# The first cross attention of a gated two-layer block: rewritten stage, weights quantised by two comparisons

## The chip, the cores and the metric
One core of one Trainium2 chip runs the whole program. The time is device microseconds for one execution; the median of 3 runs stands in the table below. The trace is one further execution, recorded by the hardware profiler.

## What is computed
Four parts follow each other; each adds tanh(gate) times its result to the rows x, of shape [4, 512, 512]. The change lies in the first part, and in the quantisation of the second part's weights, which this stage does as well:

```python
# 1: cross attention without projections of the queries; ctx is [4, 512, 128]
xn  = (x - mean(x)) / sqrt(var(x) + 1e-5)          # per row of 512
kv  = ctx @ W_k.T + b_k                            # [4, 512, 128]
out = einsum('bij,bjd->bid', xn, kv)               # the rows weigh the keys
sim = einsum('bid,bjd->bij', out, kv) * 512**-0.5
sim = (sim - mean(sim)) * rsqrt(var(sim) + 1e-6) * gamma + beta
x   = x + tanh(g_xattn[0]) * softmax(sim)
# weights of part 2 (w1 and w2, 2048 x 512 each), used as they come out of this:
m   = clip(mean(abs(w)), 1e-5)
q   = clip(round(w / m), -1, 1)                    # -1, 0 or 1, times m later
# 2: feed-forward with 8-bit activations; 3: grouped attention; 4: gated feed-forward
```

## The kernel before
The rows lie in SBUF as 16 tiles of 128 rows by 512 (`xs`), four tiles a batch. `xattn0` is one block of instruction streams, one per engine, each in program order; the engines wait for each other through semaphores, and `ffn0` begins when all of them have left the block. No planner orders the work: the order is the one in which the code issues it.

Batch 0 is peeled, and a hardware loop runs over the other three. In `head(b)` DVE takes the row statistics (`bn_stats` L430, `bn_aggr` L433), POOL forms the inverse root (L523), and DVE writes the normalised rows `xn` (L440). In `project(b)` PE forms the keys (L586), turns them (L589) and the rows (L596, f32 transposes through two PSUM banks that ACT empties, L547), and forms the outputs (L603); `similarities(b)` forms four tiles of 128 x 512 (L611). In `tail(b)` DVE takes statistics of the four similarity tiles (L448), subtracts the mean and multiplies by gamma (L455), multiplies by the inverse root and adds beta (L460), takes the maximum (L464), and, after ACT's exponentials (L554), adds the weighted result to the rows (L472). DVE does `head(b + 1)` and then `tail(b)`.

The weights come as eight chunks of 128 x 2048 f32 (`wf`). ACT sums their magnitudes, two chunks a batch (`magnitudes`, L562). When all eight are summed, DVE and PE form the two scales. Each chunk is then quantised in three passes: multiply by the inverse scale and add 1.5 * 2^23, which rounds (`scale_chunks`, L71 and L73); clip (`clip_chunks`, DVE, L79); subtract the constant and write bf16 (`store_chunks`, L87, L89, L91). `SCALED_BY` and `STORED_BY` say which engine does which chunk. `tail(3)` stands ahead of DVE's share of this; POOL's scaling of three chunks runs beside `tail(3)`.

Of the kernel before, what the change touches and what calls it, by code (L numbers as in the profile page):

```python
# [255 lines left out]
def flamingo(nc, a, out):  # L256
    ctx = ExitStack()
    with ctx:
# [17 lines left out]
        x_loaded = sem("x_loaded")  # L276
# [43 lines left out]
def xattn0(nc, a, ph, sb, ps, sem, g):  # L320
# [14 lines left out]
    W_CHUNKS = 8  # L335
# [16 lines left out]
    bn2 = t("bn2", [P, TILES, 6])
    mv2 = t("mv2", [P, TILES, 2])
    ve2 = t("ve2", [P, TILES])
    rs2 = t("rs2", [P, TILES])
    nmax = t("nmax", [P, TILES])
    esum = t("esum", [P, TILES])
    rsum = t("rsum", [P, TILES])
    wabs = t("wabs", [P, W_CHUNKS])
    b1c, b1d, b1p = t("b1c", [P, INNER // P]), t("b1d", [P, 2, INNER // P]), t("b1p", [P, 3, INNER // P], bf16)  # L360
    b1_loaded, b1_parted, b1_left, b1x_cleared = s("b1_loaded"), s("b1_parted"), s("b1_left"), s("b1x_cleared")
    wtot = t("wtot", [P, 2])
    winv = t("winv", [P, 2])

    xT_ps = [ps(f"a_xTps{k}", [P, SEQ], where=ph) for k in range(2)]
    kv_ps = ps("a_kvps", [P, SEQ], where=ph)
    o_ps = ps("a_ops", [P, SEQ], where=ph)
    sim = ps("a_sim", [P, TILES, SEQ], where=ph)

    kv_loaded, vec_loaded, w_loaded = s("kv_loaded"), s("vec_loaded"), s("w_loaded")  # L370
    x0_loaded = s("x0_loaded")
    passed = s("dve_passed")
    step = s("dve_step")
    ve_ready, rs_ready = s("ve_ready"), s("rs_ready")
    ve2_ready, rs2_ready = s("ve2_ready"), s("rs2_ready")
    xn_ready = s("xn_ready")
    kvT_done, kvT_ready, kvt_done, kv_ready = s("kvT_done"), s("kvT_ready"), s("kvt_done"), s("kv_ready")
    xT_done, xT_ready = s("xT_done"), s("xT_ready")
    o_done, oT_ready = s("o_done"), s("oT_ready")
    sim_done, sim_read = s("sim_done"), s("sim_read")  # L380
    v_ready, exp_ready = s("v_ready"), s("exp_ready")
    wabs_ready, wtot_asked, wtot_done, w_scale_ready = s("wabs_ready"), s("wtot_asked"), s("wtot_done"), s("w_scale_ready")
    chunk_stage = [s(f"chunk_stage{k}") for k in range(W_CHUNKS)]
    SCALED_BY = ("vector", "scalar", "pool", "vector", "scalar", "pool", "scalar", "pool")
    STORED_BY = ("pool", "scalar", "scalar", "pool", "scalar", "pool", "vector", "vector")
    targets = ([w1q[:, k, :] for k in range(CH)]
               + [w2q[:].rearrange("p c n -> p (c n)")[:, k * INNER:(k + 1) * INNER] for k in range(W_CHUNKS - CH)])
    chunks = [wf[:, k, :] for k in range(W_CHUNKS)]
    factors = [winv[:, k // CH:k // CH + 1] for k in range(W_CHUNKS)]

    with nc.Block() as block:

        @block.sync
        def _(sp):
            sp.dma_start(xs[:, 0:TILES, :], g["x_view"][:, 0:TILES, :]).then_inc(x0_loaded, 16)
            sp.dma_start(ident[:], a["identity"]).then_inc(consts_loaded, 16)
            sp.dma_start(gate4[:], a["gates"].rearrange("(o n) -> o n", o=1).broadcast_to([P, 4])).then_inc(consts_loaded, 16)
# [4 lines left out]
            sp.dma_start(gamma[:], a["gamma"].rearrange("(o n) -> o n", o=1).broadcast_to([P, SEQ])).then_inc(vec_loaded, 16)  # L402
            sp.dma_start(beta[:], a["beta"].rearrange("(o n) -> o n", o=1).broadcast_to([P, SEQ])).then_inc(vec_loaded, 16)
            sp.dma_start(xs[:, TILES:, :], g["x_view"][:, TILES:, :]).then_inc(x_loaded, 16)
            w1_view, w2_view = a["w1T"].rearrange("(c p) n -> p c n", p=P), a["w2T"].rearrange("(c p) n -> p c n", p=P)
            for k in range(W_CHUNKS // 2):
                if k:
                    sp.wait_ge(w_loaded, 16 * k)
                if k < 2:
                    sp.dma_start(wf[:, 2 * k:2 * k + 2, :], w1_view[:, 2 * k:2 * k + 2, :]).then_inc(w_loaded, 16)  # L410
                else:
                    sp.dma_start(wf[:, 2 * k:2 * k + 2, :].rearrange("p k (c n) -> p (k c) n", n=DIM),
                                 w2_view[:, IC // 2 * (k - 2):IC // 2 * (k - 1), :]).then_inc(w_loaded, 16)
            sp.dma_start(g["b2g"][:], a["b2"].rearrange("(o n) -> o n", o=1).broadcast_to([P, DIM])).then_inc(g["vec0_loaded"], 16)
            sp.wait_ge(b1_parted, 3)
            sp.wait_ge(b1x_cleared, 1)
            for k in range(3):
                for j in range(3):
                    row = HD * k + j
                    sp.dma_start(g["b1x"][row:row + 1, :].rearrange("o (p n) -> o p n", p=P),  # L420
                                 b1p[:, k, :]).then_inc(g["b1x_loaded"], 16)

        @block.vector
        def _(dve):
            small = Tally(step)

            def head(b, first):

                for i in range(TILES):
                    last = small.mark(nc.vector.bn_stats(bn[:, i, :], xs[:, ds(b * TILES + i, 1), :]))  # L430
                held(dve, step, last, passed)
                for i in range(TILES):
                    last = small.mark(nc.vector.bn_aggr(mv[:, i, :], bn[:, i, :]))  # L433
                dve.wait_ge(step, last)
                nc.vector.tensor_scalar(ve[:], mv[:, :, 1], EPS_IN, None, ALU.add).then_inc(ve_ready, 1)
                if not first:
                    dve.wait_ge(xT_done, b * CH)
                dve.wait_ge(rs_ready, b + 1)
                for i in range(TILES):
                    last = nc.vector.tensor_scalar(xn[:, i, :], xs[:, ds(b * TILES + i, 1), :],  # L440
                                                   mv[:, i, 0:1], rs[:, i:i + 1], ALU.subtract, ALU.mult)
                last.then_inc(xn_ready, 1)

            def tail(b):

                for i in range(TILES):
                    dve.wait_ge(sim_done, b * TILES + i + 1)
                    last = small.mark(nc.vector.bn_stats(bn2[:, i, :], sim[:, i, :]))  # L448
                held(dve, step, last, passed)
                for i in range(TILES):  # L450
                    last = small.mark(nc.vector.bn_aggr(mv2[:, i, :], bn2[:, i, :]))
                dve.wait_ge(step, last)
                nc.vector.tensor_scalar(ve2[:], mv2[:, :, 1], EPS_SIM, None, ALU.add).then_inc(ve2_ready, 1)
                for i in range(TILES):
                    nc.vector.scalar_tensor_tensor(out=v[:, i, :], in0=sim[:, i, :], scalar=mv2[:, i, 0:1],  # L455
                                                   in1=gamma[:], op0=ALU.subtract, op1=ALU.mult).then_inc(sim_read, 1)
                dve.wait_ge(rs2_ready, b + 1)
                for i in range(TILES):
                    dve.wait_ge(sim_read, b * TILES + i + 1)
                    last = small.mark(nc.vector.scalar_tensor_tensor(  # L460
                        out=v[:, i, :], in0=v[:, i, :], scalar=rs2[:, i:i + 1], in1=beta[:],
                        op0=ALU.mult, op1=ALU.add))
                    dve.wait_ge(step, last)
                    nc.vector.tensor_reduce(nmax[:, i:i + 1], v[:, i, :], axis=AX, op=ALU.max,  # L464
                                            negate=True).then_inc(v_ready, 1)
                dve.wait_ge(exp_ready, b * TILES + TILES)
                last = small.mark(nc.vector.reciprocal(rsum[:], esum[:]))
# [1593 lines left out]
```

## Time and profile before

| | us |
|---|---|
| median of 3 runs | 921.85 (921.52 to 922.08) |
| the profiled execution | 921.24, of which the recorded span is 919.3 |
| the changed block in the trace | 0.7 to 128.7 |
| busy in the whole span: PE, DVE, ACT, POOL | 674.5, 703.1, 598.3, 330.4 |

The block's end is the end of POOL's last store at L91. The first instruction of `ffn0` starts at 129.0. Times in the views are counted from the start of the span.

### The profile page before, as it was taken

The page shows a single profiled execution, that of the slowest core. Times are in us where ns is not written, and L with a number is a line of the kernel's source. Part 1 is how long each engine was busy: PE and PEld are TensorE (multiplying, and loading weights), DVE is VectorE, ACT ScalarE, POOL GpSimd, SP SyncE. Part 2 cuts the span into 40 slices and gives each one's busy share as a digit, 9 for nine tenths or more (in the row PEclk, how much of TensorE's full clock was granted, in tenths as well). Part 3 has the DMA queues.
Part 4 walks back from the last instruction along what each step waited for, and adds up shares of the span by engine and source line. Part 5 has one row for each costly group of instructions (what it writes and reads, how often), then busy time and mean ns, then how long its engine had stood idle before and what let it go on. Part 6 is the DMA issues. An engine that isn't in the chain of part 4 may idle for free. (4 is left out here: it accounts for less than half of the span.)

```text
span 919.3 us, 14368 instructions
## 1 busy us (share of the span) xinstructions
PE 674.5 (73%) x5260; PEld 374.0 (41%) x5260; DVE 703.1 (76%) x1170; ACT 598.3 (65%) x784; POOL 330.4 (36%) x353
## 2 busy tenths in 40 slices
PE   4655007676857774769989887999998477879796
PEld 2322003333323332435654555465555144545453
DVE  3886977999999999687785589476451478989884
ACT  2546428999795989378884688399554055656574
POOL 1110460343468556365283167021112013323232
PEclk9977557999797997869999998999999888989899
DMA  8710030000000000432231012022100000000001
GB/s 330 260 46 0 0 118 20 1 0 1 1 1 0 1 1 1 134 105 89 77 113 32 1 65 76 13 86 70 36 2 1 32 1 0 35 24 23 23 36 46
DMA packets 21726, 43.68 MB, mean 48 GB/s; under 512 B 3872, under 2 KB 8480, under 8 KB 20768
## 3 DMA queue, kind: packets, MB, share of 16 engines
q1 hardware_dynamic: 21664, 42.85, 13.7%
q8 instruction: 39, 0.64, 0.3%
q14 instruction: 23, 0.19, 0.1%
HBM read 38.61 MB, written 4.19 MB: 47 GB/s over the span
## 5 line engine op out<-in xcount | busy, mean ns | idle before, releaser
L1338 DVE TENSOR_REDUCE c_nmax<-c_s 128x1 f32<-128x384 f32 (+3 forms) x176 | 108.6, 633 | 83.6 <-PE c_s L1548 83.4
L1450 ACT ACTIVATE c_probs<-c_e 128x512 f32<-128x512 f32 (+1 forms) x176 | 94.4, 558 | 56.7 <-PE c_e L1578 55.6
L1046 PE MATMUL b_y<-w2q,b_q2T 128*128 128x512 bf16 x256 | 72.6, 438 | 53.5 <-ACT b_q2T L971 28.0
L1273 POOL TENSOR_TENSOR c_psum<-c_probs 128x1536 f32<-128x1536 f32 x16 | 55.8, 3490 | 155.7 <-ACT c_probs L1450 155.7
L1976 PE MATMUL d_gu<-gateq,d_xqT 128*128 128x352 bf16 x512 | 94.8, 336 | 13.4 <-DVE d_h L1777 12.4
L1545 PE MATMUL c_s<-c_kT,c_qaT 96*128 96x128 f16 (+3 forms) x256 | 73.8, 321 | 19.7 <-DVE c_nmax L1338 18.2
L1020 PE MATMUL b_up<-shared,b_xqT 128*128 128x512 bf16 x256 | 71.3, 404 | 2.6 <-ACT b_h L937 2.6
L1576 PE MATMUL c_e<-c_qaT,c_kT 98*128 98x512 f16 (+3 forms) x256 | 69.7, 306 | 4.1 <-ACT c_qaT L1437 3.6
L1905 ACT ACTIVATE d_sg<-d_gu,d_dq 128x352 f32<-128x352 f32 x64 | 35.3, 553 | 53.9 <-PE d_gu L1976 53.9
L1976 PEld LDWEIGHTS d_gu<-gateq,d_xqT 128*128 128x128 bf16 x512 | 49.8, 103 | 50.1 <-DVE d_h L1777 18.3
L1046 PEld LDWEIGHTS b_y<-w2q,b_q2T 128*128 128x128 bf16 x256 | 25.8, 108 | 92.2 <-issue 39.3
L1548 PE MATMUL c_s<-c_mask,ident_b 128*128 128x128 bf16 x256 | 53.5, 233 | 0.0
L1545 PEld LDWEIGHTS c_s<-c_kT,c_qaT 96*128 96x128 f16 x256 | 25.9, 102 | 65.5 <-DVE c_nmax L1338 38.9
L1007 PE MATMUL b_t<-ident_b,b_xq 128*128 128x128 bf16 x80 | 8.7, 251 | 58.9 <-DVE b_inv L757 45.9
L1578 PE MATMUL c_e<-ident_b,c_mask 128*128 128x128 bf16 x256 | 50.5, 223 | 0.0
L1777 DVE SCALAR_TENSOR_TENSOR d_h<-d_gu,d_dq,d_sg 128x352 f32<-128x352 f32 x64 | 37.0, 578 | 9.9 <-ACT d_sg L1905 9.5
L1999 PE MATMUL d_y<-downq,d_q2T 128*128 128x512 bf16 x176 | 41.6, 385 | 3.9 <-ACT d_q2T L1930 3.9
L230 POOL TENSOR_TENSOR c_xsin<-c_xw,ssin 128x256 f32<-128x256 f32 x32 | 32.8, 1043 | 22.5 <-DVE c_xw L214 22.5
L766 DVE SCALAR_TENSOR_TENSOR b_h<-b_h,b_nmu,b_ln_g 128x2048 f32<-128x2048 f32 x16 | 37.6, 2349 | 3.5 <-ACT b_nmu L946 3.4
L1860 POOL TENSOR_SCALAR d_q<-d_h 128x1408 bf16<-128x1408 f32 x16 | 23.0, 1438 | 47.0 <-ACT d_h L1920 46.9
L774 DVE SCALAR_TENSOR_TENSOR b_h<-b_h,b_rstd,b_ln_b 128x2048 f32<-128x2048 f32 x16 | 38.1, 2379 | 2.4 <-POOL b_rstd L876 2.4
L1020 PEld LDWEIGHTS b_up<-shared,b_xqT 128*128 128x128 bf16 x256 | 26.0, 104 | 34.0 <-issue 11.1
(233 smaller groups left out, 1849.4 us busy)
## 6 DMA issues: line engine op xcount, KB each, us to landing
c_stage<-in_gateT SPq DMA_DIRECT2D x16, 704.0 KB, 4.1
c_stage<-in_downT SPq DMA_DIRECT2D x6, 768.0 KB, 4.4
a_wf<-in_w1T SPq DMA_DIRECT2D x2, 2048.0 KB, 13.3
a_wf<-in_w2T SPq DMA_DIRECT2D x2, 2048.0 KB, 8.3
out<-xs SPq DMA_DIRECT2D x16, 256.0 KB, 2.0
xs<-in_x SPq DMA_DIRECT2D x1, 3072.0 KB, 14.8
xs<-in_x SPq DMA_DIRECT2D x1, 1024.0 KB, 5.3
a_ctxT<-in_ctxT SPq DMA_DIRECT2D x1, 1024.0 KB, 7.2
```

Source lines behind the costliest of these rows:

```text
L774: nc.vector.scalar_tensor_tensor(out=h2[:, n % H2S, :], in0=h2[:, n % H2S, :], scalar=rstd[:, n:n + 1], in1=ln_b[:], op0=ALU.mult, op1=ALU ...
L1020: nc.tensor.matmul(up_ps[k][:, m * DIM:(m + 1) * DIM], xqT[:, n % 4, c, :], w1q[:, c, at:at + DIM], start=(c == 0), stop=False)
L1046: last = nc.tensor.matmul(y_ps[:], q2T[:, n % 2, c, :], w2q[:, c, :], start=(c == 0), stop=(c == IC - 1))
L1273: nc.gpsimd.tensor_tensor(psum[:], region(slot, 0)[:, :, P:], region(slot, 1), ALU.add).then_inc(psum_ready, 1)
L1338: nc.vector.tensor_reduce(nmax[:, G % 2, i, n:n + heads], s_ps[u % 2][:, 0:heads * (i + 1) * P].rearrange("p (n k) -> p n k", n=heads), ax ...
L1450: nc.scalar.activation(probs[:, G % 2, at:at + width], e_ps[fill % 3][:, 0:width], ACT.Exp).then_inc(e_read, 1)
L1545: nc.tensor.matmul(s_ps[u % 2][:, m * width:(m + 1) * width], qaT[0:AUG, grp * GROUP + n + m, i * P:(i + 1) * P], kT[0:AUG, b % 2, grp, 0: ...
L1548: last = nc.tensor.matmul(s_ps[u % 2][:, m * width + i * P:(m + 1) * width], ident_b[:], mask[:], start=False, stop=True)
L1576: nc.tensor.matmul(e_ps[fill % 3][:, m * width:(m + 1) * width], kT[0:FULL, b % 2, grp, k * P:(k + 1) * P], qaT[0:FULL, h + m, k * P:], st ...
L1578: last = nc.tensor.matmul(e_ps[fill % 3][:, m * width:m * width + P], mask[:], ident_b[:], start=False, stop=True)
L1976: last = nc.tensor.matmul(gu_ps[k % 2][:, half, 0:PART], xqT[:, i % 2, c, :], gateq[:, c, at:at + PART], start=(c == 0), stop=(c == CH - 1))
L1999: last = nc.tensor.matmul(y_ps[:], q2T[:, c, :], downq[:, c, :], start=(c == 0), stop=(c == NC1 - 1))
```

## The change
The block is rewritten without hardware loops.

- The mean of the similarities goes away, because the keys are centred first: ACT sums the keys while it copies them, DVE subtracts the mean (`centred`), and both the values and the similarities use the centred keys. The rows are turned as they were loaded, not normalised. Their inverse deviation cancels in the second normalisation, up to the small constant, which `least` takes up.
- The variance of a similarity tile is a sum of squares by ACT (`square`).
- DVE multiplies a tile by the inverse root and gamma (`sloped`), then adds beta and takes the extreme in one instruction (`shifted`, `tensor_tensor_reduce`).
- Work on tiles is ordered by pairs, with six slots for `v`, four PSUM banks for similarities, two copies of keys, values and outputs. The fronts of the next batches are issued ahead.
- A transposed row block is emptied from PSUM 1024 wide, two instructions a batch.
- A weight becomes (w > m/2) - (w < -m/2): POOL writes the second comparison to the bf16 target (`below`), DVE the first minus it (`ternary`). ACT has no part in it. Chunks 0 to 3 need only the first scale.
- SP issues all loads at once without waits between the weight chunks, the context first, the rows by batch.

Core of the diff (added lines; those they replace are in the functions above):

```diff
+            def centred(b):
+                dve.wait_ge(kvT_ready, b + 1)
+                last = small.mark(nc.vector.tensor_scalar(kmean[:, b:b + 1], ksum[:, b:b + 1], 1.0 / SEQ, None, ALU.mult))
+                dve.wait_ge(step, last)
+                if b >= 2:
+                    dve.wait_ge(sim_done, (b - 1) * TILES)
+                nc.vector.tensor_scalar(kvcT[:, b % 2, :], kvT[:], kmean[:, b:b + 1], None, ALU.subtract).then_inc(kvc_ready, 1)
+            def variances(p):
+                dve.wait_ge(squared, 2 * p + 2)
...
+            def sloped(n):
+                dve.wait_ge(rs_ready, n // 2 + 1)
+                if n >= SLOTS:
+                    dve.wait_ge(x_ready, n - SLOTS + 1)
+                nc.vector.scalar_tensor_tensor(out=v[:, n % SLOTS, :], in0=sim[n % SIMS][:], scalar=rs[:, n:n + 1], in1=gamma,
+                                               op0=ALU.mult, op1=ALU.mult).then_inc(sim_read, 1)
+            def shifted(n):
+                dve.wait_ge(sim_read, n + 1)
+                at = v[:, n % SLOTS, :]
+                nc.vector.tensor_tensor_reduce(at, at, beta, -1.0, 3.0e38, ALU.add, ALU.min, nmax[:, n:n + 1]).then_inc(v_ready, 1)
...
+            def finished(p):
+                shares(p)        # waits for exponentials 2p and 2p+1
+                residual(2 * p)
+                residual(2 * p + 1)
...
+            def ternary(k):
+                dve.wait_ge(below_ready, k + 1)
+                nc.vector.scalar_tensor_tensor(out=targets[k], in0=wf[:, k, :], scalar=over[:, k // CH:k // CH + 1], in1=targets[k],
+                                               op0=ALU.is_gt, op1=ALU.subtract).then_inc(quantised, 1)
...
+            for b in range(BATCH):
+                variances(2 * b)
+                if b == 0:
+                    centred(1)
+                elif b + 2 < BATCH:
+                    centred(b + 2)
+                variances(2 * b + 1)
+                if b == 0:
+                    bias_parts()
+                else:
+                    finished(2 * b - 1)
+                if b == 2:
+                    weight_scale(0)
+                for p in range(2 * b, 2 * b + 2):
+                    for n in (2 * p, 2 * p + 1):
+                        sloped(n)
+                    for n in (2 * p, 2 * p + 1):
+                        shifted(n)
+                if b == 0:
+                    centred(2)
+                if b + 1 < BATCH:
+                    statistics(b + 1)
+                if b == 3:
+                    ternary(0)
+                    weight_scale(1)
+                    ternary(1)
+                finished(2 * b)
+                if b == 1:
+                    weight_sum(0)
+                if b == 2:
+                    weight_sum(1)
+            ternary(2)
+            finished(PAIRS - 1)
+            for k in range(3, W_CHUNKS):
+                ternary(k)
...
         @block.gpsimd
+            def below(k):
+                pool.wait_ge(under_ready, k // CH + 1)
+                nc.gpsimd.tensor_scalar(targets[k], wf[:, k, :], under[:, k // CH:k // CH + 1], 1.0,
+                                        ALU.is_lt, ALU.mult).then_inc(below_ready, 1)
...
+            for p in range(PAIRS):
+                pool.wait_ge(ve_ready, p + 1)
+                nc.gpsimd.tensor_tensor(rs[:, cols(p)], ve[:, cols(p)], minus_half[:, 0:2], ALU.pow).then_inc(rs_ready, 1)
+                if p == 5:
+                    below(0)
+                    below(1)
+                if p == 6:
+                    below(2)
+            for k in range(3, W_CHUNKS):
+                below(k)
...
         @block.scalar          # MAGNITUDES = (((), (0, 1)), ((2,), (3, 4)), ((5, 6), (7,)), ((), ()))
+            front_out(0)       # keys_out, rows_out(b, 0), values_out, rows_out(b, 1), outputs_out
+            for b in range(BATCH):
+                for n in range(b * TILES, (b + 1) * TILES):
+                    square(n)
+                if b == 0:
+                    act.wait_ge(consts_loaded, 16)
+                    nc.scalar.activation(gate4[:], gate4[:], ACT.Tanh).then_inc(gates_ready, 1)
+                    front_out(1)
+                if b + 2 < BATCH:
+                    keys_out(b + 2)
+                    rows_out(b + 2, 0)
+                for k in MAGNITUDES[b][0]:
+                    magnitude(k)
+                exponential(b * TILES)
+                exponential(b * TILES + 1)
+                if b + 2 < BATCH:
+                    values_out(b + 2)
+                    rows_out(b + 2, 1)
+                exponential(b * TILES + 2)
+                exponential(b * TILES + 3)
+                for k in MAGNITUDES[b][1]:
+                    magnitude(k)
+                if b + 2 < BATCH:
+                    outputs_out(b + 2)
...
         @block.tensor          # front(b): keys, turn_rows(b, 0), turn_keys, turn_rows(b, 1), outputs
+            front(0)
+            for b in range(BATCH):
+                for n in range(b * TILES, (b + 1) * TILES):
+                    similar(n)
+                if b == 0:
+                    front(1)
+                if b + 2 < BATCH:
+                    front(b + 2)
+                if b >= 2:
+                    weight_total(b - 2)
```

## Rows read from the trace of the kernel before

**Rows 1.** The page, part 1: busy time, share, instructions of each engine.
```profile
PE 674.5 (73%) x5260; PEld 374.0 (41%) x5260; DVE 703.1 (76%) x1170; ACT 598.3 (65%) x784; POOL 330.4 (36%) x353
```

**Rows 2.** Stretches of 10 us: length, busy time of each engine, granted clock, DMA.
```profile
60.00:70.00 10.00, 1.70 (x6) 0.57 (x4) 8.06 (x20) 5.47 (x8) 1.01 (x1) 0.76 0.00 0
...
110.00:120.00 10.00, 0.00 (x0) 0.00 (x0) 10.00 (x10) 5.51 (x3) 6.93 (x1) 0.50 0.00 0
120.00:130.00 10.00, 0.00 (x0) 0.00 (x0) 3.85 (x5) 0.00 (x0) 9.21 (x4) 0.50 0.01 2
```

**Rows 3.** The timeline to 80 us: start, length, engine, line, operation.
```profile
10.43 2.07 PE L586 MATMUL a_kvps<-a_ctxT,a_wkT 128*128 128x512 f32 x2 [10.43 <-DMA a_ctxT<-in_ctxT]
...
17.68 3.60 PE L603 MATMUL a_ops<-a_xT,a_kv 128*128 128x512 f32 x8
...
21.96 3.70 PE L611 MATMUL a_sim<-a_kvT,a_oT 128*128 128x512 f32 x8 [0.69 <-ACT a_oT L549]
...
42.06 2.47 DVE L430 BATCH_NORM_STATS2 a_bn<-xs 128x6 f32 x4
...
63.70 2.46 DVE L430 BATCH_NORM_STATS2 a_bn<-xs 128x6 f32 x4
...
73.63 4.54 PE L603 MATMUL a_ops<-a_xT,a_kv 128*128 128x512 f32 x8
```

**Rows 4.** Groups of instructions in 0 to 200 us: busy us, mean ns | idle before.
```profile
L562 ACT ACTIVATE a_junk<-a_wf 128x2048 bf16 (+1 forms) x8 | 15.2, 1904 | 0.6
...
L596 PE MATMUL a_xTps<-ident,a_xn 128*128 128x128 f32 x64 | 13.1, 382 | 8.2 <-DVE a_xn L440 7.9 <-ACT a_xT L547 0.3
L554 ACT ACTIVATE a_v<-a_v,a_nmax 128x512 f32<-128x512 f32 x16 | 11.5, 718 | 8.2 <-DVE a_nmax L464 8.0
...
L464 DVE TENSOR_REDUCE a_nmax<-a_v 128x1 f32<-128x512 f32 x16 | 11.0, 686 | 0.5
L472 DVE SCALAR_TENSOR_TENSOR xs<-a_v,a_rsum,xs 128x512 f32 (+1 forms) x16 | 11.0, 746 | 0.5 <-DVE a_rsum L469 0.5
L937 ACT ACTIVATE b_h<-b_up,b_dq 128x1024 f32<-128x1024 f32 x10 | 10.9, 1113 | 3.4 <-PE b_up L1022 3.4
L455 DVE SCALAR_TENSOR_TENSOR a_v<-a_sim,a_mv,a_gamma 128x512 f32<-128x512 f32 x16 | 10.9, 742 | 0.0
...
L448 DVE BATCH_NORM_STATS2 a_bn<-a_sim 128x6 f32<-128x512 f32 x16 | 9.9, 681 | 0.0
L430 DVE BATCH_NORM_STATS2 a_bn<-xs 128x6 f32 (+1 forms) x16 | 9.9, 679 | 5.0 <-DMA xs<-in_x 5.0
...
L547 ACT ACTIVATE a_xT<-a_xTps 128x512 f32<-128x512 f32 x16 | 9.3, 597 | 11.7 <-PE a_xTps L596 11.6
...
L440 DVE TENSOR_SCALAR a_xn<-xs,a_mv,a_rs 128x512 f32 (+1 forms) x16 | 7.7, 543 | 4.6 <-POOL a_rs L523 4.6
...
L554 ACT ACTIVATION_READ_ACCUMULATOR a_v<-a_v,a_nmax 128x1 f32 x16 | 3.0, 189 | 0.0
```

**Rows 5.** The timeline from 94 us, POOL, then DVE.
```profile
96.00 6.72 POOL L73 TENSOR_SCALAR a_wf<-a_wf,a_winv 128x2048 f32<-128x2048 f32 x3
113.07 13.75 POOL L91 TENSOR_SCALAR shared<-a_wf 128x2048 bf16<-128x2048 f32 x2 [10.35 <-DVE a_wf L79]
126.80 1.89 POOL L91 TENSOR_SCALAR w2q<-a_wf 128x2048 bf16<-128x2048 f32 x1
...
99.15 1.74 DVE L460 SCALAR_TENSOR_TENSOR a_v<-a_v,a_rs,a_beta 128x512 f32<-128x512 f32 x1
...
120.85 2.35 DVE L89 TENSOR_SCALAR w2q<-a_wf 128x2048 bf16<-128x2048 f32 x2
```

**Rows 6.** Single lines of the program: duration in ns, least/median/most, and starts.
```profile
L73 POOL TENSOR_SCALAR a_wf<-a_wf,a_winv x3: 1969/2394/2395, 96.0 to 100.3; 128x2048 f32<-128x2048 f32 x3
...
L766 DVE SCALAR_TENSOR_TENSOR b_h<-b_h,b_nmu,b_ln_g x16: 2339/2344/2403, 150.7 to 354.6; 128x2048 f32<-128x2048 f32 x16
```

**Rows 7.** The page, part 5: the costliest two-tensor operation on POOL.
```profile
L1273 POOL TENSOR_TENSOR c_psum<-c_probs 128x1536 f32<-128x1536 f32 x16 | 55.8, 3490 | 155.7 <-ACT c_probs L1450 155.7
```

More of the change, by code:

```diff
@@ L376, in xattn0 @@
[L376 to L383, printed above, removed]
@@ L425, in _ @@
             small = Tally(step)
[L427 to L433, printed above, removed]
-                dve.wait_ge(step, last)
[L435 to L451, printed above, removed]
-                dve.wait_ge(step, last)
[L453 to L467, printed above, removed]
-                dve.wait_ge(step, last)
-                last = small.mark(nc.vector.tensor_scalar(rsum[:], rsum[:], gate4[:, 0:1], None, ALU.mult))
-                dve.wait_ge(step, last)
-                for i in range(TILES):
-                    last = small.mark(nc.vector.scalar_tensor_tensor(
-                        out=xs[:, ds(b * TILES + i, 1), :], in0=v[:, i, :], scalar=rsum[:, i:i + 1],
-                        in1=xs[:, ds(b * TILES + i, 1), :], op0=ALU.mult, op1=ALU.add))
@@ new lines, in statistics @@
+            def statistics(b):
+                dve.wait_ge(rows_loaded[b], 16)
+                for n in range(b * TILES, (b + 1) * TILES):
+                    last = small.mark(nc.vector.bn_stats(bn[:, n, :], xs[:, n, :]))
+                dve.wait_ge(step, last)
+                for n in range(b * TILES, (b + 1) * TILES):
+                    last = small.mark(nc.vector.bn_aggr(mv[:, n, :], bn[:, n, :]))
+                dve.wait_ge(step, last)
+                c = slice(b * TILES, (b + 1) * TILES)
+                nc.vector.tensor_scalar(least[:, c], mv[:, c, 1], SPREAD, SPREAD * EPS_IN, ALU.mult, ALU.add).then_inc(least_ready, 1)
@@ new lines, in shares, with residual @@
+            def shares(p):
+                c = cols(p)
+                dve.wait_ge(exp_ready, 2 * p + 2)
+                last = small.mark(nc.vector.reciprocal(rsum[:, c], esum[:, c]))
+                dve.wait_ge(step, last)
+                last = small.mark(nc.vector.tensor_scalar(share[:, c], rsum[:, c], gate4[:, 0:1], None, ALU.mult))
+                dve.wait_ge(step, last)
+            def residual(n):
+                nc.vector.scalar_tensor_tensor(out=xs[:, n, :], in0=v[:, n % SLOTS, :], scalar=share[:, n:n + 1], in1=xs[:, n, :],
+                                               op0=ALU.mult, op1=ALU.add).then_inc(x_ready, 1)
@@ new lines, in outputs_out, with square, exponential @@
+                nc.scalar.activation(oT[:, b % 2, :], o_ps[:], ACT.Copy).then_inc(oT_ready, 1)
+            def square(n):
+                act.wait_ge(sim_done, n + 1)
+                if n:
+                    act.wait_ge(squared, n)
+                nc.scalar.activation(junk2[:], sim[n % SIMS][:], ACT.Square, accum_out=squares[:, n:n + 1]).then_inc(squared, 1)
+            def exponential(n):
+                act.wait_ge(v_ready, n + 1)
+                at = v[:, n % SLOTS, :]
+                nc.scalar.activation(at, at, ACT.Exp, bias=nmax[:, n:n + 1], scale=-1.0, accum_out=esum[:, n:n + 1]).then_inc(exp_ready, 1)
@@ L580, in _, with keys, turn_keys @@
         @block.tensor
         def _(pe):
-            def project(b, first):
-                if not first:
+            def keys(b):
+                if b:
                     pe.wait_ge(kv_ready, b)
-                nc.tensor.matmul(kv_ps[:], wkT[:], ctxT[:, ds(b * SEQ, SEQ)], start=True, stop=True).then_inc(kvT_done, 1)
+                nc.tensor.matmul(kv_ps[:], wkT[:], ctxT[:, b * SEQ:(b + 1) * SEQ], start=True, stop=True).then_inc(kvT_done, 1)
+            def turn_keys(b):
+                pe.wait_ge(kvc_ready, b + 1)
@@ L600, in project, with similar @@
                     pe.wait_ge(oT_ready, b)
                 for c in range(CH):
[L602 to L603 removed]
+                    last = nc.tensor.matmul(o_ps[:], kv[:, b % 2, c, :], xT[:, c, :], start=(c == 0), stop=(c == CH - 1))
                 last.then_inc(o_done, 1)
[L606 removed]
+            def similar(n):
+                b, i = n // TILES, n % TILES
@@ L607, in similarities @@
                 pe.wait_ge(oT_ready, b + 1)
-                for i in range(TILES):
-                    if not first:
-                        pe.wait_ge(sim_read, b * TILES - TILES + i + 1)
-                    nc.tensor.matmul(sim[:, i, :], oT[:, i * P:(i + 1) * P], kvT[:], start=True, stop=True).then_inc(sim_done, 1)
-            pe.wait_ge(kv_loaded, 48)
-            pe.wait_ge(consts_loaded, 32)
-            project(0, True)
-            similarities(0, True)
-            with pe.Fori(0, BATCH - 1) as b:
-                project(b + 1, False)
-                similarities(b + 1, False)
@@ new lines, in weight_total, with front @@
+            def weight_total(w):
+                pe.wait_ge(wtot_ready, w + 1)
+                pe.wait_ge(kv_ready, BATCH)
+                nc.tensor.matmul(kv_ps[:, w:w + 1], ones[:], wtot[:, w:w + 1], start=True, stop=True).then_inc(wtot_done, 1)
+            pe.wait_ge(kv_loaded, 48)
+            pe.wait_ge(ident_loaded, 16)
+            def front(b):
+                keys(b)
+                turn_rows(b, 0)
+                turn_keys(b)
+                turn_rows(b, 1)
+                outputs(b)
```

281 lines of the change are left out of this document (135 added, 146 removed).

## The prediction
> **What bounds the kernel now.** I read the page's busy shares first. No engine is busy for more than 76% of the span (DVE) [rows 1], so the bound changes from stage to stage, and the stage that changes has to be read by itself. The table of stretches shows two kinds of time in it. In the batches DVE is busy 8.06 of 10 us and PE 1.70 [rows 2]; the timeline gives their period, 63.70 - 42.06 = 21.6 us from one batch's row statistics to the next [rows 3]. Per batch DVE's seven groups of 512-wide work make about 4 x (0.68 + 0.54 + 0.68 + 0.74 + 0.74 + 0.69 + 0.75) = 19.3 us by their means [rows 4], so DVE bounds the batches. At the end comes the quantisation. From 110 us DVE is busy 10.00 of 10 us, then 3.85, while POOL is busy 9.21 [rows 2]. The timeline says why: two POOL stores take 13.75 us, from 113.07 to 126.8; DVE's last instruction of the block ends at 120.85 + 2.35 = 123.2; POOL's third store, alone, takes 1.89 us, and its end, 128.7, is the block's [rows 5]. The second of the two stores began after that, so the first took 13.75 - 1.9 = 11.9 us for work that costs 1.89 alone, because DVE worked back to back beside it. The block thus ends with POOL locked out and finishing alone.
>
> **What the lock does.** The new form puts two-input DVE work beside POOL work, so this price decides. L460 has two SBUF inputs; beside POOL's L73 one of them took 1.74 us, while L455, with one input in PSUM, keeps a mean of 0.74 [rows 4, 5]. L73 itself took 1.969 us the first time and 2.394 after that [rows 6]. 2.394 - 1.969 is nearly the part of a 512-wide operation that streams. Both read as exclusion: one runs, the other stands, and only some 0.2 us of start-up overlaps. Serial prices follow. A POOL pass of 2048 costs about 1.83 us (1.89 alone), a 512-wide two-input DVE operation 0.68, a 2048-wide one 2.27 (2.344 alone, less start-up) [rows 4 to 6].
> The Trainium skill (SBUF — State Buffer, Who interferes with whom) states this as a rule: a DVE instruction with two SBUF inputs and a POOL instruction that reads SBUF take turns, for the whole instruction. By that rule, eight `below` and eight `ternary` are hardly parallel; the trace agrees (1.74 against 0.74 us). Without it the sum would be the one of rival C.
>
> **Part by part, before the last stage.** Removed from DVE: similarity statistics (16 x 0.68), the normalised rows (16 x 0.54), the separate maximum (16 x 0.69) [rows 4]: 30.6 us. Added: centring (4 x about 0.8, from a 512-wide L440 plus a small operation), 16 accumulator outputs, and the eight `ternary`, 18.2 us, in place of 12 DVE passes (L73, L79, L89) at 1.2 us (L89, 2.35 for two [rows 5]), 14.1 us. So DVE's own work shrinks by only some 20 us (30.6 + 14.1 - 3.2 - 2.7 - 18.2), and less of it may be seen, since ACT gains work: 16 squares at 0.9 us (0.718 + 0.189, taken from the exponential; the lower bound is a copy from PSUM plus the accumulator, 0.6 + 0.19) [rows 4]. ACT loses its six quantisation passes, some 11 us.
>
> *First similarity.* Now at 21.96 [rows 3]. The context was behind the rows in the queue and landed at 10.43; it will be ahead, and PE begins near 8. Keys 2.2, half of the rows turned 1.8 (16 transposes of mean 0.38 overlap to about 0.22 each) [rows 4], keys turned, the other half 1.8, one 1024-wide copy 1.1 on each side of it (L937) [rows 4], outputs 3.6, copy 0.6: about 20.5. The fourth square ends near 25.1. DVE's start waits for the tanh of the gates, which is behind those squares, so 25.3 is DVE's start.
>
> *Squares of batch 1.* The chain runs through PE and ACT. 25.3 -> keys out 0.9, DVE centres 0.8, keys and rows turned 1.8, copy 1.1: 29.9 -> outputs 3.6, keys(2) 1.0: 34.5 -> ACT keys and rows out 2.1: 36.7 -> two exponentials 1.8 (DVE finished them by 31), values 0.6, rows 1.1: 40.2. PE then makes outputs(2) and the similarities by 47.5, because these stand behind front(2) in its queue. ACT is later: two exponentials 1.8, two magnitudes 4.2 (1.904 + 0.189 each), outputs 0.6, four squares 3.6: 50.4. DVE idles about 7 us here.
>
> *Squares of batch 2.* 50.4 -> keys out 0.9; DVE centres, then variances, `finished(1)` 1.9, two `sloped` and two `shifted` 2.8: 56.9 -> ACT exponentials to 58.0, values and rows out 1.7: 59.7. From here ACT needs 1.8 + 4.2 + 0.6 to 66.3, and PE 3.6 at full clock, 4.54 at the mixed clock that L603 met once after an idle stretch [rows 3], plus one similarity of 0.95: 64.3 to 66. Four squares: 70.3. A slower clock is hidden under ACT here.
>
> **The last stage, from 70.3.** DVE now has a queue of work without gaps, each term with its serial price. Not through the shared port: eight `sloped` (one input in PSUM) 8 x 0.68 = 5.4, the last row statistics 3.2, five pairs of shares 2.3, variances 0.5, scales 1.2: 12.6. Through it: eight `shifted` at 0.85 = 6.8, ten `residual` at 0.68 = 6.8, eight `ternary` 18.2: 31.8. POOL's `below` 4 to 7 come when DVE has nothing else than port work: 4 x 1.83 = 7.3. `below` 0 to 3 (7.3 in all) lie beside `sloped` and statistics for about half; I count 3.5. Sum 55.2, end 125.5.
> `shifted` is an operation that no row shows. Its main pass is bounded below by L460's 0.68 and above by L460 and L464 apart, 0.74 + 0.69; I take the lower plus 0.17 for an accumulator read, as ACT's 0.189. With the upper, ten of them on the path cost 5.8 more; with nothing for the accumulator, 1.7 less. `below` has no row either, as a comparison: from 1.83 (L91, the same widths and types) up to 2048/1536 x 3.49 = 4.65 (L1273, two tensors [rows 7]). I take 1.83, being the row of the same operation.
>
> **Forecast.** The block ends at 125.5 instead of 128.7: 3.2 us less. Everything behind the block keeps its order and tiles; I cost it at nothing. PE stands idle before `ffn0` both times and the granted clock is at 1.2 GHz there already (0.50) [rows 2]. So the profiled execution goes from 921.24 to 918.0, and the median, 0.6 higher than the profiled one, from 921.85 to 918.6. About 0.2% (1.8 us) is what can be told from no change here. My own range for this case is 915 to 921.5: the ends of `shifted`, start-up 1 us either way, `below` 0 to 3 shown from 1 to 6 us.
>
> **Rivals.**
> A. *POOL's comparison is dear* (the other side). A compare is slower on POOL than the add and multiply of L91. All eight `below` lie under the lock or ahead of a waiting `ternary`, so each us of extra length costs near 8 us. At 3.3 us each, the middle of the bounds, that is 8 x 1.5 = 12 more: 930.6. It decides from 1.83 + (1.8 + 3.2)/8 = 2.5 us; beneath that the result is not slower by 0.2%. For it: no comparison of POOL in the trace. Against: L91 and L73 do two arithmetic operations with different outputs at the same price. Chance 0.13.
> B. *The early chain is longer.* ACT and PE lead in the first 70 us; one exponential, copy or wait more in each of the two cycles, and idle time that I packed too tightly, give 3 to 6 us: 921.6 to 924.6, say 922.5. For it: many crossings of semaphores; against: DVE's idle time there absorbs what DVE does. Chance 0.16.
> C. *POOL runs beside DVE after all.* Then `below` costs nothing, 10.8 us less: about 908. Rows 5 speak against it. Chance 0.07.
> D. *The fused add and extreme runs at half rate.* 0.53 us more for each `shifted`, ten on the path: 923.9. For it is only that L460 with two f32 inputs has no accumulator; L766 at 2.344 us for 2048 elements shows full rate without one [rows 6]. Chance 0.06.
> The Trainium skill has a rule of this kind (Vector Engine (DVE) Microarchitecture Reference, Points that are easy to get wrong: "`S2S2D2_STT` with two non-bf16 SBUF sources halves throughput"). Taken for plain operations the trace disagrees (2.344 us is one element a cycle of 1.04 ns); with an accumulator no run shows it yet.
> E. *It doesn't do what it says*: PE still waits long, DVE does not shed its gaps, and the block ends within 1.8 us of before. Chance 0.06, at 921.5.
>
> **Chances.** Forecast 0.52, of which faster 0.42, same 0.10. B: 0.04 faster, 0.07 same, 0.05 slower. C faster 0.07. A slower 0.13. D 0.02 same, 0.04 slower. E 0.01 faster, 0.03 same, 0.02 slower. Sums: faster 0.54, same 0.22, slower 0.24. The likeliest is 918.6. The range goes down to 913, half way to C, since overlap of `below` could be better than counted, and up to 926, past B and D and short of most of A.
>
> **What would show it right or wrong.** The timeline should show the first similarity near 20.5, square 7 ending near 50, square 11 near 70, DVE without a gap over 1 us after that, and the last `ternary` near 125. Pairs of `below` and `ternary` should add up to about 4.1 us each, with PE idle and DVE and POOL never both streaming. `below` alone in its line should show a least duration near 1.9, `shifted` 0.74 plus a short read. If `below` shows over 2.5 us, A holds and the forecast fails; if DVE ends `ternary` 7 before 120, C; if square 11 ends after 74, B.

## The result, and the profile after

| | median us | ratio to before, same chip (95% interval) | block ends at, us |
|---|---|---|---|
| before | 921.68 (4 runs) | | 128.7 |
| changed | 938.13 (4 runs) | 1.0179 (1.0161 to 1.0197) | 145.3 |

I forecast 918.6 in a range of 913 to 926; the change makes the kernel 1.8% slower. The profiled execution took 938.19 us against 921.24, 16.95 more, and the block ends 145.3 - 128.7 = 16.6 us later. So the loss lies inside the rewritten block, and what stands behind it moved by no more than 0.4 us.

Where it goes is seen first in the stretches of 10 us of the changed kernel (length, busy time of PE, its weight loads, DVE, ACT, POOL, then granted clock and DMA), to be laid beside [rows 2]:

```profile
60.00:70.00 10.00, 6.27 (x15) 2.79 (x14) 4.22 (x14) 7.79 (x14) 2.30 (x3) 0.84 0.00 0
70.00:80.00 10.00, 7.15 (x8) 2.13 (x8) 9.97 (x18) 5.38 (x11) 10.00 (x2) 0.55 0.00 0
...
110.00:120.00 10.00, 0.00 (x0) 0.00 (x0) 9.96 (x4) 0.00 (x0) 10.00 (x2) 0.50 0.00 0
120.00:130.00 10.00, 0.00 (x0) 0.00 (x0) 9.93 (x4) 0.00 (x0) 10.00 (x3) 0.50 0.00 0
130.00:140.00 10.00, 0.00 (x0) 0.00 (x0) 10.00 (x5) 0.00 (x0) 5.36 (x1) 0.50 0.00 0
```

DVE looks as busy as before, but a count of 4 instructions in 10 us says that it isn't working: an instruction that waits for the port counts as busy. POOL, at 10.00 with two instructions, sets the pace. The timeline of the changed kernel gives both sides (start, length, engine, line):

```profile
69.10 15.23 POOL L565 TENSOR_SCALAR shared<-a_wf,a_under 128x2048 bf16<-128x2048 f32 x2 [1.44 <-DVE a_under L508]
...
70.29 3.94 DVE L468 CUSTOM_DVE_ANT_0 a_v<-a_v,c_turned 128x512 f32<-128x512 f32 x1
74.16 0.08 DVE L468 DVE_READ_ACCUMULATOR2_ANT a_nmax<- 128x1 f32 x1
74.16 0.68 DVE L468 CUSTOM_DVE_ANT_0 a_v<-a_v,c_turned 128x512 f32<-128x512 f32 x1
...
80.22 4.13 DVE L439 TENSOR_SCALAR a_least<-a_mv 128x4 f32<-128x4 f32 x1
81.67 2.68 DVE L473 RECIPROCAL a_rsum<-a_esum 128x2 f32<-128x2 f32 x1
...
103.92 31.44 POOL L565 TENSOR_SCALAR w2q<-a_wf,a_under 128x2048 bf16<-128x2048 f32 x4 [1.25 <-DVE a_under L508]
...
106.07 0.16 DVE L473 RECIPROCAL a_rsum<-a_esum 128x2 f32<-128x2 f32 x1
106.26 6.93 DVE L475 TENSOR_SCALAR a_share<-a_rsum,gate 128x2 f32<-128x2 f32 x1
113.23 5.70 DVE L479 SCALAR_TENSOR_TENSOR xs<-a_v,a_share,xs 128x512 f32<-128x512 f32 x2
118.86 2.34 DVE L513 SCALAR_TENSOR_TENSOR shared<-a_wf,a_over,shared 128x2048 bf16<-128x2048 f32 x1
...
136.17 9.13 DVE L513 SCALAR_TENSOR_TENSOR w2q<-a_wf,a_over,w2q 128x2048 bf16<-128x2048 f32 x4
```

L565 is `below`. Single durations of its line in the changed kernel (ns, least/median/most, first and last start), against 1969/2394/2395 in [rows 6]:

```profile
L565 POOL TENSOR_SCALAR shared<-a_wf,a_under x4: 7156/7308/8053, 69.1 to 95.5; 128x2048 bf16<-128x2048 f32 x4
L565 POOL TENSOR_SCALAR w2q<-a_wf,a_under x4: 7151/7530/9253, 103.9 to 128.2; 128x2048 bf16<-128x2048 f32 x4
```

The shortest comparison pass takes 7.15 us where I had put 1.83. Everything else came near its mark: first similarity at 20.38 (20.5 forecast), the squares of batch 1 done at 47.6 (50.4), those of batch 2 (square 11 is the last of them) at 66.7 (70.3), `shifted` 0.68 with an accumulator read of 0.08, `ternary` 2.34.

### The profile page after: what moved, and what is told of

The parts are those of the page before. It is cut to its first block and busy times, and to the rows that moved or that the text cites. A ratio compares the mean times of both kernels' runs of the same rounds, so it can differ in the third digit from the quotient of the medians.

```text
span 936.4 us, 14250 instructions
## 1 busy us (share of the span) xinstructions
PE 675.8 (72%) x5262; PEld 371.5 (40%) x5262; DVE 715.6 (76%) x1142; ACT 595.4 (64%) x806; POOL 367.0 (39%) x355
## 5 line engine op out<-in xcount | busy, mean ns | idle before, releaser
L1120 PE MATMUL b_up<-shared,b_xqT 128*128 128x512 bf16 x256 | 73.2, 412 | 2.4 <-ACT b_h L1037 2.4
L1029 ACT ACTIVATE b_xqT<-b_t 128x640 bf16<-128x640 bf16 x16 | 11.1, 697 | 66.9 <-PE b_t L1107 66.9
L1678 PE MATMUL c_e<-ident_b,c_mask 128*128 128x128 bf16 x256 | 50.4, 222 | 0.0
L1877 DVE SCALAR_TENSOR_TENSOR d_h<-d_gu,d_dq,d_sg 128x352 f32<-128x352 f32 x64 | 37.0, 578 | 10.2 <-ACT d_sg L2005 9.8
## 6 DMA issues: line engine op xcount, KB each, us to landing
a_wf<-in_w2T SPq DMA_DIRECT2D x2, 2048.0 KB, 20.5
```

What stands on the lines that cost most here:

```text
L1120: nc.tensor.matmul(up_ps[k][:, m * DIM:(m + 1) * DIM], xqT[:, n % 4, c, :], w1q[:, c, at:at + DIM], start=(c == 0), stop=False)
L1678: last = nc.tensor.matmul(e_ps[fill % 3][:, m * width:m * width + P], mask[:], ident_b[:], start=False, stop=True)
L1877: nc.vector.scalar_tensor_tensor(out=h[:, i % 2, k * PART:(k + 1) * PART], in0=gu_ps[k % 2][:, 1, 0:PART], scalar=dq1[:, i:i + 1], in1=sg[ ...
```

## The experiments

Three theories were set against each other. Theory 1: one price is wrong, the comparison on POOL. Theory 2: handing the shared port back and forth costs, whatever POOL does. Theory 3: the rewritten attention loses. The first four kernels ran on one chip, where before took 922.84.

**e1_pool_add.** The comparison becomes an addition.

```diff
 nc.gpsimd.tensor_scalar(targets[k], wf[:, k, :], under[...], 1.0,
-                        ALU.is_lt, ALU.mult)
+                        ALU.add, ALU.mult)
```

> The changed kernel with the comparison in POOL's `below` replaced by an addition, same operands, types and lock; the weights of the second part are then not the reference's. Theory 1 (the comparison itself is dear on POOL, 7.15 us at the least in the trace of the changed kernel against 1.89 for the add and multiply of L91; nothing else failed): `below` falls to 1.9 us alone, the block ends near 121 us instead of 145.3 (my 125.5 less the 4 us by which the squares of batch 2 came earlier), and the time is 914 us. Theory 2 (the handing over of the shared port between POOL and DVE is what costs, small DVE instructions included, whatever POOL does): `below` gets cheaper but gaps and stretched DVE instructions remain, and the block ends at 128 or later, 921 us or more. Theory 3 (the rewritten attention loses the time): 930 us or more.

Measured: 914.97 us, ratio 0.9908 (0.9891 to 0.9926). The same line in this kernel, and its timeline behind square 11:

```profile
L565 POOL TENSOR_SCALAR w2q<-a_wf,a_under x4: 1966/2396/4072, 95.8 to 104.1; 128x2048 bf16<-128x2048 f32 x4
```

```profile
82.53 1.97 POOL L565 TENSOR_SCALAR shared<-a_wf,a_under 128x2048 bf16<-128x2048 f32 x1
82.62 1.89 DVE L455 SCALAR_TENSOR_TENSOR a_ve<-a_squares,a_least 128x2 f32<-128x2 f32 x1 [0.86 <-ACT c_xsin L611]
...
95.76 10.77 POOL L565 TENSOR_SCALAR w2q<-a_wf,a_under 128x2048 bf16<-128x2048 f32 x4 [8.29 <-DVE a_under L508]
...
98.11 1.75 DVE L475 TENSOR_SCALAR a_share<-a_rsum,gate 128x2 f32<-128x2 f32 x1
...
112.64 9.13 DVE L513 SCALAR_TENSOR_TENSOR w2q<-a_wf,a_over,w2q 128x2048 bf16<-128x2048 f32 x4
```

One operation code of one instruction moves the time by 23 us, and the sign of the change with it. The block ends at 121.8. Theory 1 holds in its number (914); theories 2 and 3 fall as the main cause.

**e2_dve_both.** POOL has no part in the quantisation.

```diff
 def ternary(k):
+    nc.vector.tensor_scalar(targets[k], wf[:, k, :], under[...], 1.0, ALU.is_lt, ALU.mult).then_inc(below_ready, 1)
     dve.wait_ge(below_ready, k + 1)
```

> The changed kernel with both comparisons on DVE: `below` is a DVE tensor_scalar right ahead of each `ternary`, POOL has only the inverse roots. Theory 1: no POOL pass and no lock, DVE gets 8 more passes, at 1.22 us each if a comparison runs at the rate of L79 or 2.3 us at one element a cycle; from 66.6 us 44.4 us of DVE work plus 9.8 (or 18.4) end the block near 121 (or 129), 914 (or 922) us. Theory 2 says the same as or better than the run with the addition, since the lock is gone: 8 us or more below it. Theory 3: 930 us or more.

Measured: 912.01 us, ratio 0.9892 (0.9867 to 0.9917), block end 118.4. The timeline's pair for one chunk:

```profile
104.01 1.28 DVE L512 TENSOR_SCALAR w2q<-a_wf,a_under 128x2048 bf16<-128x2048 f32 x1
105.33 2.35 DVE L515 SCALAR_TENSOR_TENSOR w2q<-a_wf,a_over,w2q 128x2048 bf16<-128x2048 f32 x1
```

The comparison that takes POOL 7.15 us takes DVE 1.28. The kernel is 3 us faster than e1, with intervals that overlap, where theory 2 asked for 8 or more; but square 11 is done at 65.5 here and at 68.4 in e1, and from there to the block's end the two need 52.9 and 53.4 us. That is not the price of the lock, since the work differs. DVE does eight passes of 1.28 us more in e2, 10.2 us, and in e1 its instructions behind square 11 last 11.1 us longer than they do alone, because they wait for POOL (L475 1.75 instead of 0.23 us, for one). So the eight short POOL passes cost about what the forecast had put for them, 7.3 + 3.5 = 10.8 us, and little is left over for a price of handing the port back and forth.

**e3_old_quant** and **e4_old_attn** do one part each, as nearly as can be. In e3 `ternary` and `below` become the three passes of before:

```diff
-nc.vector.scalar_tensor_tensor(out=targets[k], in0=wf[:, k, :], scalar=over[...], in1=targets[k], op0=ALU.is_gt, op1=ALU.subtract)
+nc.scalar.activation(wf[:, k, :], wf[:, k, :], ACT.Copy, scale=winv[...], bias=MAGIC)      # 0, 1, 3, 4, 6, 7; POOL 2, 5
+nc.vector.tensor_scalar(wf[:, k, :], wf[:, k, :], MAGIC + 1.0, MAGIC - 1.0, ALU.min, ALU.max)
+nc.gpsimd.tensor_scalar(targets[k], wf[:, k, :], -MAGIC, 1.0, ALU.add, ALU.mult)          # 0, 1, 3, 4, 6; ACT 2, 5, 7
```

> One part undone: the rewritten attention of the changed kernel, the quantisation in the three passes of before (multiply and add, clip, subtract), chunk 2's and 5's first pass on POOL, the others on ACT; POOL writes chunks 0, 1, 3, 4, 6, ACT the others, DVE clips all eight at 1.22 us. Theory 1: the rewritten attention is worth its forecast and more, DVE has 26.2 + 9.8 us from 66.6, ACT and POOL finish after its last clip: block end near 108, time 901 us. Theory 3: the block ends no earlier than 128, 921 us or more.

Measured: 905.65 us, ratio 0.9817 (0.9801 to 0.9833), block end 109.6; theory 3 falls, and the time is 4.7 us over theory 1's. The three passes are shared out otherwise than in the kernel before: there DVE does 12 of the 24 (two multiply and add, eight clip, two store), here only the eight clips. The run is thus not the rewritten attention alone.

In e4 the kernel before gets `over` and `under` in place of `winv`, and:

```diff
-scale_chunks(...); clip_chunks(...); store_chunks(...)
+for k in range(W_CHUNKS):     # POOL; then DVE's second comparison on each
+    nc.gpsimd.tensor_scalar(targets[k], wf[:, k, :], under[...], 1.0, ALU.is_lt, ALU.mult)
```

> The other part alone: the attention of the kernel before, the weights by two comparisons, `below` of all eight chunks on POOL from the scales at 91.5 us, `ternary` on DVE after the last batch's tail. Theory 1: eight passes of 7.15 us on POOL from 96 us with DVE's work between them end near 160, and the ternary passes left over end near 170 to 175: 964 us. Theory 2: the passes on POOL are stretched by the handing over and not long themselves: 935 to 945 us. Theory 3 (the comparisons are cheap, the attention loses): 925 us or less.

Measured: 955.06 us, ratio 1.0346 (1.0328 to 1.0363). From the end of its timeline:

```profile
129.81 28.58 POOL L534 TENSOR_SCALAR w2q<-a_wf,a_under 128x2048 bf16<-128x2048 f32 x4
...
137.00 6.67 DVE L516 SCALAR_TENSOR_TENSOR w2q<-a_wf,a_over,w2q 128x2048 bf16<-128x2048 f32 x1 [0.48 <-POOL w2q L534]
144.14 6.66 DVE L516 SCALAR_TENSOR_TENSOR w2q<-a_wf,a_over,w2q 128x2048 bf16<-128x2048 f32 x1 [0.48 <-POOL w2q L534]
```

The attention, with the three passes shared out anew, gives 922.84 - 905.65 = 17.2 us; the two comparisons alone cost 955.06 - 922.84 = 32.2. Together that is +15.0, and the change shows +16.5. How much of the 17.2 belongs to the sharing out no run shows; four passes at 1.2 us fewer on DVE are 4.8 us of its work. The rows of e4 hold something else. Four passes take 28.58 us, 7.15 each, as if nobody were beside them, and each period of 7.15 also holds a `ternary`. Its 6.67 us are 4.4 of waiting and 2.3 of work, and it ends before the pass beside it does. So theory 1 had POOL's passes right (they end at 158.4, near 160) and missed by 9 us because a pass and a `ternary` overlap: only one `ternary` is left behind the last pass.

**e5_forms** and **e9_forms2** are price lists of POOL's pass with DVE held back.

```diff
+form = {3: (edge, 1.0, ALU.is_gt, ALU.mult), 4: (edge, 1.0, ALU.min, ALU.mult), 5: (edge, 1.0, ALU.subtract, ALU.mult),
+        6: (-0.016, 1.0, ALU.is_lt, ALU.mult), 7: (edge, None, ALU.is_lt, None), ...}[k]
+nc.gpsimd.tensor_scalar(targets[k], wf[:, k, :], form[0], form[1], form[2], form[3])
```

> Price list of POOL's one-tensor pass, 128 x 2048 f32 to bf16: the changed kernel in which DVE waits until all eight passes are done, so that chunks 3 to 7 run without DVE beside them. Chunk 3: greater-than and multiply; 4: minimum and multiply; 5: subtract and multiply; 6: less-than against a constant instead of a column; 7: less-than alone; 0 and 1 as in the changed kernel, 2 add. Weights of the second part are not the reference's. If every comparison is dear (theory 1): 3, 6 and 7 take 7.15 us, 4 and 5 1.9. If it is the pair less-than with multiply: 7 falls to 2 us. If it is the column operand: 6 falls to 2 us. If it is anything but plain arithmetic: 4 is dear as well. No time is expected of it but these durations.

> More of the price list: as in the run of five forms, DVE waits, chunks 3 to 7 run alone on POOL, the weights of the second part are not the reference's. Chunk 3: multiply and multiply; 4: add and add; 5: multiply and add; 6: multiply alone; 7: maximum alone; 2: add and multiply. If only the pairs of one addition and one multiplication have the short pass: 5 takes 1.97 us, 3 and 4 7.1, 6 and 7 5.4 as less-than alone did. If the short pass belongs to additions and multiplications in any number: 3, 4, 5 and 6 take 2 us, 7 takes 5.4.

POOL's timeline in the first list (chunks 3, 4, 5, 6, 7), one line for each chunk, then in the second (3 to 7):

```profile
97.86 7.17 POOL L574 TENSOR_SCALAR shared<-a_wf,a_under 128x2048 bf16<-128x2048 f32 x1 [7.21 <-DVE a_under L508]
105.02 7.16 POOL L574 TENSOR_SCALAR w2q<-a_wf,a_under 128x2048 bf16<-128x2048 f32 x1
...
112.17 7.18 POOL L574 TENSOR_SCALAR w2q<-a_wf,a_under 128x2048 bf16<-128x2048 f32 x1
...
119.43 7.09 POOL L574 TENSOR_SCALAR w2q<-a_wf 128x2048 bf16<-128x2048 f32 x1
126.61 5.44 POOL L572 TENSOR_SCALAR w2q<-a_wf,a_under 128x2048 bf16<-128x2048 f32 x1
```

```profile
100.40 1.97 POOL L574 TENSOR_SCALAR shared<-a_wf,a_under 128x2048 bf16<-128x2048 f32 x1 [7.21 <-DVE a_under L508]
102.34 7.18 POOL L574 TENSOR_SCALAR w2q<-a_wf,a_under 128x2048 bf16<-128x2048 f32 x1
109.51 1.97 POOL L574 TENSOR_SCALAR w2q<-a_wf,a_under 128x2048 bf16<-128x2048 f32 x1
111.46 5.45 POOL L572 TENSOR_SCALAR w2q<-a_wf,a_under 128x2048 bf16<-128x2048 f32 x1
116.89 5.46 POOL L572 TENSOR_SCALAR w2q<-a_wf,a_under 128x2048 bf16<-128x2048 f32 x1
```

The starts of passes that follow each other lie as far apart as the durations say (102.34, 109.51, 111.46). So comparison was too narrow a word. Multiply-multiply and multiply-add have the short pass (1.97), as add-multiply has (1.97 in e1). Add-add, subtract-multiply, minimum-multiply and both comparisons with a multiply take 7.1 to 7.2, with a constant as with a column. One operation alone takes 5.45, even a multiply. None of the readings in e5's expectation had subtraction dear, and both of my readings in e9's expectation fell in part: multiply-multiply is short, add-add is not.

**e6_order** and **e8_share_stt** test how the lock is held.

```diff
 if b == 3:                                   # e6
+    finished(6)
+    finished(7)
     ternary(0)
     weight_scale(1)
```

```diff
-nc.vector.tensor_scalar(share[:, c], rsum[:, c], gate4[:, 0:1], None, ALU.mult)                        # e8
+nc.vector.scalar_tensor_tensor(out=share[:, c], in0=rsum[:, c], scalar=gate4[:, 0:1], in1=ones[:, 0:2], op0=ALU.mult, op1=ALU.mult)
```

> The changed kernel with DVE's `finished(6)` and `finished(7)` ahead of `ternary(0)` and the second scale, so that nothing but `ternary` runs beside the last four comparison passes. Theory 1b: a comparison pass of 7.15 us holds the port's read side for its first 4.4 us only (in the changed kernel DVE's waiting two-input instructions end 4.9 us after the pass begins), so that a `ternary` fits into the rest, while a DVE tensor_scalar of 128 x 2 waits the whole pass (6.94 us at L475). Then four passes end 28.6 us after the scale (near 108.5), `ternary` 7 2.3 us after them: block end near 139.5, 932 us. If a pass and a `ternary` exclude each other for their whole lengths: four times 9.3 plus the rest, block end near 149, 941 us. If the order is indifferent: 938 us.

Measured: 937.73 us (before 921.85), ratio 1.0164 (1.0139 to 1.0189): no difference from the change that can be told. The block ends at 143.7, not 139.5. Its timeline, read line by line:

```profile
108.92 9.26 POOL L566 TENSOR_SCALAR w2q<-a_wf,a_under 128x2048 bf16<-128x2048 f32 x1 [5.94 <-DVE a_under L508]
118.17 8.85 POOL L566 TENSOR_SCALAR w2q<-a_wf,a_under 128x2048 bf16<-128x2048 f32 x1
...
108.81 2.35 DVE L513 SCALAR_TENSOR_TENSOR shared<-a_wf,a_over,shared 128x2048 bf16<-128x2048 f32 x1
117.66 2.34 DVE L513 SCALAR_TENSOR_TENSOR shared<-a_wf,a_over,shared 128x2048 bf16<-128x2048 f32 x1
```

From 119.9 on each `ternary` takes its 4.4 + 2.3 inside a pass of 7.15, as theory 1b says, and the passes start at 108.9, where the expectation had them (108.5; in the changed kernel 103.9). But the four passes take 32.4 us and not 28.6: the first two find a `ternary` running when they start (108.81 and 117.66) and last 9.26 and 8.85. The overlap was right; that a running `ternary` holds the next pass off was left out of this sum, and what DVE saves is spent on the later start.

> The changed kernel with one DVE instruction of 128 x 2 in another form: the product of the reciprocal and the gate as scalar_tensor_tensor times a column of ones (two SBUF inputs) instead of tensor_scalar. Theory 1b: L475 in its two blocked places waits 4.4 us instead of 6.9, the residuals then fall into the free rest of the same pass, and each of the two places gives back 2.5 to 6 us: 926 to 933 us. If small instructions wait for the whole pass whatever their form: 938 us.

Measured: 934.00 us, ratio 1.0140 (1.0117 to 1.0164). The lines in its timeline, against 31.44, 6.93 and 5.70 in the changed kernel:

```profile
103.87 34.90 POOL L566 TENSOR_SCALAR w2q<-a_wf,a_under 128x2048 bf16<-128x2048 f32 x4 [1.25 <-DVE a_under L509]
...
106.21 4.33 DVE L475 SCALAR_TENSOR_TENSOR a_share<-a_rsum,gate,ones 128x2 f32<-128x2 f32 x1
110.58 1.41 DVE L480 SCALAR_TENSOR_TENSOR xs<-a_v,a_share,xs 128x512 f32<-128x512 f32 x2
```

An instruction on 128 x 2 elements takes 4.3 us in the two-input form and 6.9 as a tensor_scalar. The duration is as expected; the time is just outside the forecast 926 to 933, and its interval touches that of the change (1.0161 to 1.0197). DVE is past each of the two places 6.9 us sooner, yet the block ends at 141.1 instead of 145.3: the four passes now take 34.90 us instead of 31.44, since more of them find a `ternary` running, and the last `ternary` stands behind them.

**e7_placed**, **e7b_placed**, **e10_placed2**: the version that the runs point to, e3 with the passes placed by what they block. POOL has add or multiply forms only.

```diff
 if p == 5:                     # POOL
-    scale(2)
+    for k in range(CH): scale(k)
-if b == 2: weight_scale(0)     # DVE; the second scale one phase earlier
+if b >= 2: weight_scale(b - 2)
# ACT: scale 4 to 7, store 1 to 5 (e10: 0 to 5); DVE: all clips, store 6 and 7; POOL: store 0 (e10: none)
```

> Candidate for the best: the rewritten attention with the three passes of the old quantisation, placed by what the lock costs. POOL multiplies and adds chunks 0 to 3 right after the first scale, beside `sloped` and the row statistics, and stores chunk 0; the second scale is taken a batch phase earlier; ACT scales chunks 4 to 7 and stores 1 to 5; DVE clips all and stores 6 and 7. By the busy sums DVE has 26.2 + 9.8 + 2.4 us from 66 and up to 4 us of lock, ACT 8 x 0.9 + 4 x 1.95 + 5 x 1.9 from 79: block end near 106, 902 us, against 905.7 for the run with the old quantisation. If POOL's four passes block DVE for their whole lengths (theory 2): 4 x 1.9 more, 908 us or more.

Measured: 897.85 us, ratio 0.9731 (0.9707 to 0.9756). It beats both kernels, and e3 by more than the intervals; the forecast was 902.

> The placed three-pass variant once more on the same chip as the run beside it, as its comparison: 897.9 us.

> The placed three-pass variant with POOL's one store moved to ACT. In that variant the store ran at 92.2 to 95.0 and DVE's product of 128 x 2 beside it took 1.67 us instead of 0.23 and its clip before waited. Taking it away gives DVE back about 1.5 us, as DVE has no gap from there to the end; ACT gets 1.9 us more and ends with DVE near 106: 896.5 us against 897.9. If ACT becomes last: 898 us.

Measured on one chip (before 923.40): 896.82, ratio 0.9718 (0.9701 to 0.9734), and 898.37, ratio 0.9726 (0.9710 to 0.9744). The store on ACT gives nothing. DVE's 1.67 us instruction is back to 0.23, but ACT is now last, the second case of the expectation: it ends at 104.6 and DVE at 103.3, and DVE's first instruction behind the block waits idle for 1.62 us, against 0.3 in e7b.

## Why the prediction was wrong

- **`below` at 1.83 us is the step that failed.** I took L91's price "being the row of the same operation". It was the same instruction with other operation codes, and on POOL the codes decide: 7.15. The dear end of my bounds, 4.65 from L1273, was too low as well, since it came from a row of another instruction. Rival A was this mechanism, at a chance of 0.13, and its threshold of 2.5 us told the sign. Its price, 8 us for each us of extra length, would have made 5.3 x 8 = 42 us; e1 against the changed kernel shows 23.
- **Why 23 and not 42.** The lock was only half understood. The forecast let a pass and a `ternary` exclude each other. For passes of 1.9 us that serves: with the addition the block ended at 121.8; my 125.5, less the 1.9 us by which that run's squares were early, is 123.6. In that run even a two-input instruction of 128 x 2 lasts to the end of the pass beside it (82.62 + 1.89 = 84.51, 82.53 + 1.97 = 84.50). Beside a 7.15 us pass a two-input DVE instruction waits only 4.4 us and works in the rest. What waits for the whole is tensor_scalar: L439 ends at 80.22 + 4.13 = 84.35, the second pass at 69.10 + 15.23 = 84.33. The sum of what DVE's instructions last beyond their length alone, behind square 11, is 36.5 us in the changed kernel and 11.1 in e1. The difference, less the 1.7 us by which the changed kernel's square 11 is earlier, is 23.7, and the ends of the blocks lie 23.5 apart.
- **The Trainium skill's rule** (SBUF — State Buffer, SBUF: two separate sides) that the loser is blocked for the whole instruction holds here for tensor_scalar (6.93 us), and for two-input instructions beside a pass of 1.97 us, but not for two-input instructions beside a pass of 7.15 us (4.33 us, e8), which end before the POOL instruction does. The Trainium skill's remark (same title, Who interferes with whom) that the second input of these comes through the shared read interface fits that; it gives no time.
- **The early chain** was right in shape and 3.6 us too long at square 11. A square costs 0.79 (0.60 + 0.19), my lower bound, not 0.9; the 1024-wide copy 1.02, not 1.11. The outputs of batch 3 took 6.6 us, at a granted clock of 0.50 (1.2 GHz) from 55 to 60 us, where I had 3.6 to 4.54 and all of it hidden behind ACT; ACT waited 1.34 us for them. Rival B fell.
- **`shifted`** costs 0.68 + 0.08, under my 0.85: full rate, with the accumulator, so rival D fell. The Trainium skill's line on two f32 sources (Vector Engine (DVE) Microarchitecture Reference, Points that are easy to get wrong) names the instruction form `S2S2D2_STT`. `shifted` is recorded as CUSTOM_DVE_ANT_0, so no run here shows that form with an accumulator; without one the trace disagrees (L766, 2.344 us).
- **The rewritten attention** was worth more than the whole forecast of 3.2 us: 17.2 us (e3, with the passes shared out anew). I had summed it with a quantisation that, even with cheap passes, is dearer in DVE and port time than the three passes.

## What to carry to other kernels

On POOL price an instruction by its pair of operation codes, never by its name and shape; a comparison belongs on DVE (1.28 us against 7.15 here) unless a run shows otherwise. Beside a long POOL pass, count what each small DVE instruction waits for, and choose its form by that. When a change has two parts, run each alone first: here one gave some 17 us and the other took 32, and the sum hid both.

## What the runs showed that I had not expected

- POOL's tensor_scalar of 128 x 2048, f32 to bf16: 1.97 us for add-multiply, multiply-add, multiply-multiply; 7.1 to 7.2 for five other pairs; 5.45 for one operation alone. The Trainium skill (GPSIMD Engine Reference, Performance versus the Vector engine) gives 1.03 cycles an element for at most two operations. At the 1.2 GHz of the same section that is 1.76 us for 2048 elements, an estimate, which fits the first price alone.
- A DVE instruction that waits for the port is shown as busy. 128 x 2 elements took 6.93 us, and DVE read 99% busy with four instructions in 10 us.
- Why a two-input DVE instruction gets through 4.4 us into a pass of 7.15 us is open; no run varied the output's width or type. Open too is whether a reciprocal waits for POOL. The one that lasted 2.68 us ended with the tensor_scalar in front of it (84.35), and may only have stood behind it; at 106.07, about when the next pass got its turn, one took 0.16.
